# Attention of a two-layer transformer kernel: normalization of each score tile moved behind the next tile's row maxima, three PSUM regions for scores, one bank for transposes

## What is computed

```python
# layer 0: 16 heads of q, k, v; causal
scores = jnp.einsum('bhqd,bhkd->bhqk', q, k) * scale
scores = jnp.where(causal, scores, jnp.finfo(scores.dtype).min)
probs = jax.nn.softmax(scores, axis=-1)
attn = jnp.einsum('bhqk,bhkd->bhqd', probs, v)
# layer 1: 16 heads of q, one k and one v for all, no mask
scores = jnp.einsum('bhqd,bkd->bhqk', q, k) * SCALE
attn = jax.nn.softmax(scores.astype(jnp.float32), axis=-1)
out = jnp.einsum('bhqk,bkd->bhqd', attn, v)
```

## Time and profile before

| | us |
|---|---|
| device time, median of five runs | 13053.91 |
| the five runs | 12818.4 to 13098.67 |
| the profiled execution, device time | 12700.41 |
| its span on the slowest core (core 1) | 12698.9 |
| spans of the eight cores | 12643.5 to 12698.9 |
| attention of layer 0 (first scores to last cast of OT) | 1311.4 to 3442.6 |
| attention of layer 1 | 7126.6 to 9940.5 |

### The profile page before, as it was taken

One profiled execution on the slowest core, in us unless ns is written; L12 is line 12 of the kernel. 1 busy time (PEld: TensorE's weight loads), 2 busy tenths in 40 slices (PEclk: granted clock), 3 DMA queues, 4 the chain that ended last, 5 costly groups with the idle time before them and its releaser, 6 DMA issues. The chain is left out here.

```text
span 12698.9 us, 112380 instructions; the slowest of 8 cores (12643.5 to 12698.9 us)
## 1 busy us (share of the span) xinstructions
PE 7415.4 (58%) x35408; PEld 3432.6 (27%) x35408; DVE 4428.7 (35%) x8280; ACT 2475.1 (19%) x4202; POOL 135.0 (1%) x233
## 2 busy tenths in 40 slices
PE   1399433333379997281814644444444679997881
PEld 0144111111134443140412222222222334443340
DVE  4411444444414445708022344444444211111002
ACT  2100233333201112202121133333333000000000
POOL 0000000000000000000000000000000000000000
PEclk9999655555589998595956755555555789998995
DMA  1123000000132332141333100000000232223444
GB/s 50 48 55 57 19 7 7 10 7 7 28 86 48 59 60 44 36 81 35 72 118 104 35 7 7 7 7 6 5 7 4 45 78 50 53 52 78 93 90 165
DMA packets 426230, 581.35 MB, mean 46 GB/s; under 512 B 257200, under 2 KB 347312, under 8 KB 401456
## 3 DMA queue, kind: packets, MB, share of 16 engines
q0 software_dynamic: 75216, 237.39, 10.9%
q1 hardware_dynamic: 350432, 336.77, 8.3%
HBM read 655.71 MB, written 155.71 MB: 64 GB/s over the span
## 5 line engine op out<-in xcount | busy, mean ns | idle before, releaser
L636 PE MATMUL SCA<-P 128*128 128x512 bf16 x896 | 425.7, 559 | 1548.8 <-ACT P L86 1521.0
L86 DVE TENSOR_TENSOR P<-P 128x512 f32<-128x512 f32 (+6 forms) x700 | 691.4, 988 | 1674.3 <-DMA P<-g_hb 1603.0
L86 ACT ACTIVATE P<-SCA,st 128x1024 bf16<-128x1024 f32 (+1 forms) x512 | 515.8, 1007 | 3233.6 <-DVE st L86 3233.6
L781 PE MATMUL OT<-P 128*128 128x512 bf16 x1664 | 625.4, 555 | 734.3 <-DVE P L86 560.6
L607 PE MATMUL PP<-identS,P 128*128 128x128 bf16 x6656 | 732.3, 292 | 533.4 <-DVE P L86 532.6
L488 PE MATMUL QP<-P 128*128 128x512 bf16 x4224 | 961.2, 393 | 24.6 <-DMA P<-wqk 13.1
L607 PEld LDWEIGHTS PP<-identS,P 128*128 128x128 bf16 x6656 | 626.7, 134 | 854.7 <-issue 839.6
L86 DVE TENSOR_TENSOR st<-st 128x1 f32<-128x1 f32 x1632 | 259.4, 159 | 1404.4 <-ACT P L86 1214.1
L1160 PE MATMUL F1G<-P 128*128 128x512 bf16 x2816 | 627.4, 384 | 175.9 <-DVE P L86 117.2
L1250 PE MATMUL F1D<-P 128*128 128x512 bf16 x2816 | 619.2, 382 | 111.2 <-SPq L1215 111.2
L894 PE MATMUL F0P<-P 128*128 128x512 bf16 x2816 | 638.6, 380 | 67.3 <-DMA P<-w 67.3
(11 more groups left out here) (86 smaller groups left out, 6664.0 us busy)
## 6 DMA issues: line engine op xcount, KB each, us to landing
P<-w POOLq DMA_DIRECT2D x22, 2048.0 KB, 28.0
P<-w2p POOLq DMA_DIRECT2D x32, 1408.0 KB, 10.3
P<-wgu POOLq DMA_DIRECT2D x44, 1024.0 KB, 9.4
P<-wd POOLq DMA_DIRECT2D x32, 1408.0 KB, 10.2
P<-x SPq DMA_DIRECT2D x32, 1024.0 KB, 4.9
gn_hb<-P SPq DMA_DIRECT2D x176, 128.0 KB, 1.7
P<-gn_hb SPq DMA_DIRECT2D x176, 128.0 KB, 2.0
hf_h<-P SPq DMA_DIRECT2D x44, 512.0 KB, 6.0
```

What stands on the lines that cost most here:

```text
L86: ins = real(*args, **kw)
L636: ins = t.matmul(scslice(c, qt), QH[h % 2][:, qt * 128:(qt + 1) * 128], k.Bp[:, kbase + c * 512: kbase + c * 512 + 512], start=True, stop= ...
L781: ins = t.matmul(OT[:], VH[h % 2][:, kt * 128:(kt + 1) * 128], PT[:, kt * 512:(kt + 1) * 512], start=(kt == 0), stop=(kt == ktn - 1))
```

## The change

Four things are rewritten in `phase_att`, for both layers. The score regions: three PSUM tensors of two banks (SR0 to SR2) that are handed out in a ring, one per two chunks, so a tile of one or two chunks takes one region and one exponential, and a larger one two. PP is half as large, one bank, so each block of transposes waits until the block before it has been copied out. On DVE the sum, reciprocal and scaling are a function `do_rzpn`, called for tile qt - 1 after the maxima and `negm` of tile qt (of which there are two now), with the copy of block 1 of the same tile qt - 1 right behind it, and the cast of OT comes one tile later (qt % 4 == 1). On ACT the copy of block 0 of tile qt - 1 stands ahead of the exponential of tile qt.

```diff
-        negm = k.st1[:, 0:1]; za = k.st1[:, 1:2]; zb = k.st1[:, 2:3]
+        negm_b = [k.st1[:, 0:1], k.st1[:, 6:7]]
+        za = k.st1[:, 1:2]; zb = k.st1[:, 2:3]
...
-        def haf(qt):
-            n = nchf(qt)
-            return (n + 1) // 2, n - (n + 1) // 2
-
-        with self.nc.psum_tensor(f"SCA{L}", [128, 1024], F32) as SCA, \
-             self.nc.psum_tensor(f"SCB{L}", [128, 1024], F32) as SCB, \
-             self.nc.psum_tensor(f"PP{L}", [128, 2048], BF16) as PP, \
+        def nregf(qt):
+            return 1 if nchf(qt) <= 2 else 2
+
+        regs_of = {}
+        rr = 0
+        for h in range(HEADS):
+            for qt in range(NT):
+                n = nregf(qt)
+                regs_of[(h, qt)] = [rr, (rr + 1) % 3][:n]
+                rr = (rr + n) % 3
+
+        with self.nc.psum_tensor(f"SR0{L}", [128, 1024], F32) as SR0, \
+             self.nc.psum_tensor(f"SR1{L}", [128, 1024], F32) as SR1, \
+             self.nc.psum_tensor(f"SR2{L}", [128, 1024], F32) as SR2, \
+             self.nc.psum_tensor(f"PP{L}", [128, 1024], BF16) as PP, \
              self.nc.psum_tensor(f"OT{L}", [128, 512], F32) as OT:
-            pph = [PP[:, 0:1024], PP[:, 1024:2048]]
-
-            def scslice(c, qt):
-                ha, hb = haf(qt)
-                if c < ha:
-                    return SCA[:, c * 512:(c + 1) * 512]
-                return SCB[:, (c - ha) * 512:(c - ha + 1) * 512]
+            SCR = [SR0, SR1, SR2]
+
+            def scslice(h, qt, c):
+                rg = regs_of[(h, qt)][c // 2]
+                return SCR[rg][:, (c % 2) * 512:(c % 2 + 1) * 512]

             def transp(t, h, qt, ppq):
                 nkb = nchf(qt) * 4
                 PSB = PSBs[qt % 2]
                 k.wt(t, f"a{L}pn_{h}_{qt}")
                 for b in range((nkb + 7) // 8):
-                    half = b % 2
-                    if half in ppq:
-                        k.wt(t, ppq[half])
+                    if ppq:
+                        for m in ppq[0]:
+                            k.wt(t, m)
                     j0, j1 = b * 8, min(nkb, b * 8 + 8)
                     for j in range(j0, j1):
-                        ins = t.transpose(pph[half][:, (j - j0) * 128:(j - j0 + 1) * 128],
+                        ins = t.transpose(PP[:, (j - j0) * 128:(j - j0 + 1) * 128],
                                           PSB[:, j * 128:(j + 1) * 128], k.ident[:])
                     k.bump(ins, "sT", mark=f"a{L}tpb_{h}_{qt}_{b}")
-                    ppq[half] = f"a{L}pte_{h}_{qt}_{b}"
+                    nm = "S" if b % 2 == 0 else "V"
+                    ppq[:] = [[f"a{L}pte{nm}_{h}_{qt}_{b}"]]
                 k.marks[f"a{L}tp_{h}_{qt}"] = k.marks[f"a{L}tpb_{h}_{qt}_{(nkb-1)//8}"]
...
             def tenf(t):
-                ppq = {}
-                lastA = None
-                lastB = None
+                ppq = []
+                regfree = {}
                 for h in range(HEADS):
                     k.wt(t, f"a{L}qv_{h}")
                     for qt in range(NT):
-                        ha, hb = haf(qt)
+                        nch = nchf(qt)
                         kbase = h * 2048 if L == 0 else 0
-                        if lastA is not None:
-                            k.wt(t, lastA)
-                        for c in range(ha):
-                            ins = t.matmul(scslice(c, qt),
-                                           QH[h % 2][:, qt * 128:(qt + 1) * 128],
-                                           k.Bp[:, kbase + c * 512: kbase + c * 512 + 512],
-                                           start=True, stop=True)
-                            k.bump(ins, "sT", mark=f"a{L}scc_{h}_{qt}_{c}")
-                        lastA = f"a{L}expA_{h}_{qt}"
-                        if hb:
-                            if lastB is not None:
-                                k.wt(t, lastB)
-                            for c in range(ha, ha + hb):
-                                ins = t.matmul(scslice(c, qt),
+                        regs = regs_of[(h, qt)]
+                        for i, rg in enumerate(regs):
+                            if rg in regfree:
+                                k.wt(t, regfree[rg])
+                            for c in range(2 * i, min(nch, 2 * i + 2)):
+                                ins = t.matmul(scslice(h, qt, c),
                                                QH[h % 2][:, qt * 128:(qt + 1) * 128],
                                                k.Bp[:, kbase + c * 512: kbase + c * 512 + 512],
                                                start=True, stop=True)
                                 k.bump(ins, "sT", mark=f"a{L}scc_{h}_{qt}_{c}")
-                            lastB = f"a{L}expB_{h}_{qt}"
+                            regfree[rg] = f"a{L}exp_{h}_{qt}_{i}"
                         if qt > 0:
                             transp(t, h, qt - 1, ppq)
                             if (qt - 1) % 4 == 3:
                                 self._att_pv(t, L, h, (qt - 1) // 4, causal, VH, PT, OT)
...
+            def do_rzpn(v, h, qt):
+                nch = nchf(qt)
+                nreg = nregf(qt)
+                if nreg == 2:
+                    k.wt(v, f"a{L}exp_{h}_{qt}_1")
+                    ins = v.tensor_tensor(zs, za, zb, OP.add)
+                else:
+                    k.wt(v, f"a{L}exp_{h}_{qt}_0")
+                    ins = v.tensor_copy(zs, za)
+                k.bump(ins, "sV")
+                k.wtv(v, "sVa", k.cnt["sVa"])
+                ins = v.reciprocal(rz, zs)
+                k.bump(ins, "sV", mark=f"a{L}rz_{h}_{qt}")
+                k.wt(v, f"a{L}rz_{h}_{qt}")
+                PSB = PSBs[qt % 2]
+                ins = v.tensor_scalar_mul(PSB[:, 0:nch * 512], PSB[:, 0:nch * 512], rz)
+                k.bump(ins, "sV", mark=f"a{L}pn_{h}_{qt}")

             def vecf(v):
                 for h in range(HEADS):
@@ -663,12 +680,13 @@
                         off = qt % 4
                         for c in range(nch):
                             k.wt(v, f"a{L}scc_{h}_{qt}_{c}")
-                            sl = scslice(c, qt)
+                            sl = scslice(h, qt, c)
                             if causal and c == nch - 1:
                                 v.tensor_tensor(sl, sl, k.msk()[:, off * 512:(off + 1) * 512], OP.add)
                             ins = v.tensor_reduce(ngp[c], sl, AX, OP.max, negate=True)
                         k.bump(ins, "sV")
                         k.wtv(v, "sVa", k.cnt["sVa"])
+                        negm = negm_b[qt % 2]
                         if nch == 1:
                             ins = v.tensor_copy(negm, ngp[0])
                         elif nch == 2:
@@ -681,29 +699,16 @@
                             v.tensor_tensor(negm, ngp[2], ngp[3], OP.min)
                             ins = v.tensor_tensor(negm, negm, tmp, OP.min)
                         k.bump(ins, "sV", mark=f"a{L}neg_{h}_{qt}")
-                        ha, hb = haf(qt)
-                        if hb:
-                            k.wt(v, f"a{L}expB_{h}_{qt}")
-                            ins = v.tensor_tensor(zs, za, zb, OP.add)
-                        else:
-                            k.wt(v, f"a{L}expA_{h}_{qt}")
-                            ins = v.tensor_copy(zs, za)
-                        k.bump(ins, "sV")
-                        k.wtv(v, "sVa", k.cnt["sVa"])
-                        ins = v.reciprocal(rz, zs)
-                        k.bump(ins, "sV", mark=f"a{L}rz_{h}_{qt}")
-                        k.wt(v, f"a{L}rz_{h}_{qt}")
-                        PSB = PSBs[qt % 2]
-                        ins = v.tensor_scalar_mul(PSB[:, 0:nch * 512], PSB[:, 0:nch * 512], rz)
-                        k.bump(ins, "sV", mark=f"a{L}pn_{h}_{qt}")
                         if qt > 0:
-                            self._ptevac_v(v, L, h, qt - 1, nchf, pph, PT)
-                        if qt % 4 == 0 and qt >= 4:
+                            do_rzpn(v, h, qt - 1)
+                            self._ptevac_v(v, L, h, qt - 1, nchf, PP, PT)
+                        if qt % 4 == 1 and qt >= 5:
                             g = qt // 4 - 1
                             k.wt(v, f"a{L}pv_{h}_{g}")
                             ins = v.tensor_copy(k.A[:, h * 2048 + g * 512: h * 2048 + g * 512 + 512], OT[:])
                             k.bump(ins, "sV", mark=f"a{L}oev_{h}_{g}")
-                    self._ptevac_v(v, L, h, NT - 1, nchf, pph, PT)
+                    do_rzpn(v, h, NT - 1)
+                    self._ptevac_v(v, L, h, NT - 1, nchf, PP, PT)
...
             def scaf(sc):
                 for h in range(HEADS):
                     for qt in range(NT):
-                        ha, hb = haf(qt)
+                        nch = nchf(qt)
+                        regs = regs_of[(h, qt)]
                         PSB = PSBs[qt % 2]
+                        if qt > 0:
+                            self._ptevac_s(sc, L, h, qt - 1, nchf, PP, PT)
```

(21 more changed lines are left out.)

18 lines of the change are left out of this document (10 added, 8 removed).

## The result

The changed kernel took 13363.85 us (median of 6 runs, 13076.94 to 13610.18), the kernel before, beside it and earlier, 12974.72 (median of 10, 12670.45 to 13224.35). The ratio is 1.0294 with a 95% interval of 1.0172 to 1.0417. It became slower, as forecast (13460, range 13150 to 13620; 3.2% on the sum's own scale); the interval lies above 1, but it begins at 1.7%, so the times alone don't settle that the loss is over 2%.

A forecast was written before the change was run, and what follows sets the result against it. A loop of waits, not an engine, was taken to bound the attention stages. Layer 0's +163 us and layer 1's +249, together +412, added to the median 13053.9 gave 13466, rounded to 13460, range 13150 to 13620.

The forecast's parts named there:

- The removed wait: On DVE before the small operations: the 2.88 us wait for ACT's exponential becomes 0.17, -2.71 us per four-chunk tile.
- The new wait: On DVE before its copy: waiting out the same tile's transposes through one bank takes 3.77 us instead of 0.11, +3.66.
- The tile: In the attention loop, a four-chunk tile costs +0.95 us, making the layer 1 period 10.1 us; three chunks again +0.95.
- The third region off the path: On PE: the third score region removes a wait for ACT that had 4 us to spare, so gains nothing.
- The head's end: At each head's last tile, normalized alone: 6.6 us in layer 1, 7.8 in layer 0, so +4.4 and +5.6.
- The product: At the other three P V products of a layer 1 head: length unchanged, cast a tile later, +0.2 us each.
- The sum: Over both attention stages: layer 0 +163 us, layer 1 +249, together +412, or 13112 on the profiled scale, 3.2% more.
- The sign that I had named for a wrong forecast: In the profile after: a rising granted clock of the attention stages would show the forecast wrong.
- The rival in which PE wakes up: In both attention stages: PE at its faster level shortens transposes and products, total -168 us, 12532 profiled scale; chance 5%.
- The ring of banks pays: In attention: DVE's copy wait stays hidden, only removed waits count, -1127 us, 11573 on the profiled scale; chance 3%.
- The smaller loss: In attention: copy wait near 3.05 us, products at 5.4, about +172 us, 12872 on the profiled scale; chance 6%.
- the late scores: In attention tiles: the third chunk misses its 1.8 us slack, 1.5 us more per tile, +530, near 13990; chance 4%.

The follow-up runs named there:

- DVE's order put back: The changed kernel with DVE's scaling, copy and cast in their earlier order, one transpose bank kept: layer 0 2076.0 us, layer 1 2842.9, whole median 13122.61.
- two banks: The changed kernel with two transpose banks, two score regions and ACT's exponential ahead of its copy: layer 0 2304.0 us, layer 1 2678.5.
- the ring of two: The changed kernel with two score regions instead of three, nothing else: layer 0 2403.2 us, layer 1 3115.0, whole 13513.83 (median of two).
- the copy a tile later: Changed kernel with two transpose banks and score regions, two buffered score tiles, DVE's copy and product a tile later, scores ahead, undrained heads: 11503.73 us, ratio 0.868.

## Why the prediction was right

Point by point, by its own steps.

- The removed wait. I had -2.71 us a tile and DVE's waits for ACT nearly gone; 43.2 us are left of 1214.1. Right, but for a mis-sized 0.07 us: the sum of the two halves follows the small operations before it with no gap of 0.17 (four in one run at 8813.18), so the wait of 2.88 became the usual gap of 0.10 between instructions.
- The new wait. I had 3.77 us, added up from the earlier trace rows; it is 3.75 in the tile shown, and 1413.0 / 382 = 3.70 over all copies, of three chunks too (3.32 there, the 0.43 less that I had). One term has a slip that did no harm: eight transposes at 1.86 / 16 are 0.93 us and not 0.83, which would have made the sum 3.67. What eight more cost is 1.86 - 1.01 = 0.85 us, so 2.04 - 0.85 = 1.19 for the last step, and 8817.95 to 8819.14 is 1.19. DVE's order put back takes it away and restores 9.1 us a tile, two banks make 2.29 of it. Shown by both.
- The tile: +0.95 us forecast, period 10.1. It is 10.00 against 9.13, so +0.87, the 0.07 above less; the tile ahead of it in the same stretch took 10.18. For tiles of one and two chunks I had waits for scores of 1.4 and 1.85 us; they are 1.44 and 1.86.
- The third region off the path. Right for the gain that the change could hope for: PE's wait fell by 1387 us and no tile of layer 1 got shorter. But not for the new order, where it covers 0.1 us a tile in layer 1 and up to 1.7 in layer 0. With the ring of two those show.
- The head's end. I had a wait of 0.7 us for exponential 15, then 3.77 again. DVE's rows of the changed kernel at the end of a head of layer 1, which answer to the earlier trace rows:

```profile
9917.16 0.69 DVE L86 COPY P<-PP 128x1024 bf16<-128x1024 bf16 x1 [3.75 <-PE PP L614]
9918.60 0.16 DVE L86 TENSOR_TENSOR st<-st 128x1 f32<-128x1 f32 x1 [0.74 <-ACT P L86]
...
9919.27 0.75 DVE L86 TENSOR_SCALAR P<-P,st 128x2048 bf16<-128x2048 bf16 x1 [0.17 <-DVE st L86]
9923.77 0.69 DVE L86 COPY P<-PP 128x1024 bf16<-128x1024 bf16 x1 [3.75 <-PE PP L614]
9930.77 0.69 DVE L86 CAST P<-OT 128x512 bf16<-128x512 f32 x1 [6.30 <-PE OT L788]
```

  0.74 us for ACT, 3.75 for PE, and 9917.16 to 9923.77, copy to copy, is 6.61 (6.6 forecast, 2.2 before). At a head's start the third chunk is waited for 0.72 us (0.6 forecast).
- The product. I kept its length and added 0.2 us. In layer 1 the maxima behind it wait 5.9 to 6.6 us for scores, where the cast had waited 6.3 on average, and the cast comes a tile later without a wait. Right.
- The sum. +163 and +249 us forecast, +165 and +246 measured on core 1. So near a hit is in part luck: a group of four tiles with its product grew by 3.7 us on average in layer 1 (43.9 to 47.6 from cast to cast) where the terms give 4.0, and the start and end of a head took that back (8.1 us for what is left of a head, 7.55 by the terms). Layer 0's terms were not all read one by one. The time on the medians' scale, 13460, came out 96 us too high; 79 of that is the scale, since the kernel before, with five more runs, has a median of 12974.72 and not 13053.91. The nearness of a median is luck too: single times of either kernel lie over 530 us apart, more than the effect. What the forecast rests on is the 411 us of the stages.
- The sign that I had named for a wrong forecast, a granted clock that rises, was there in part: 0.63 in layer 1 after 0.58. It changed nothing on the path. Eight transposes still take 1.01 us at their usual pace, and the products' waits are as long as before. The rival in which PE wakes up fell with that; it had asked for about 0.88. The other sign, maxima that wait for scores, was badly put: they wait 690 us in all, but where the sum has it, behind products, in tiles of one and two chunks and at a head's start.
- The ring of banks pays: fell, and for the reason given. By the Trainium skill (Perfetto Trace Analysis, section Matmuls), independent groups of matmuls should rotate through PSUM banks so that the evacuation overlaps the next group's matmuls. The runs agree for the transposes: with one bank ACT's copy stands between two blocks and costs 1.46 us a tile where DVE waits for it. They also show what the rule leaves open: with the order put back the same single bank cost 29 us in a whole stage, since the evacuation was off the path.
- The smaller loss and the late scores fell: the copy waited 3.32 us or more in all of layer 0 and 3.64 or more in all of layer 1, and the maxima found their scores ready in the middle of a group of four-chunk tiles.

## What to carry to other kernels

A deferred step takes its consumers with it: when a scaling moves one tile later, the copy that needs its transposes must move too, or the engine pays PE's whole turn in the place of ACT's. Write down for each engine, for one period, what it produced last and what it asks for next; the ask should lie a period behind the thing asked for, on every engine. And buy PSUM banks where a wait stands on the path: here the third score region took away 1387 us of PE's waiting that no tile of layer 1 had paid for, and the bank it took from the transposes cost 1.46 us in each tile of four chunks once DVE waited for them.

## What the runs showed of the hardware

The same product of sixteen 128x512 matmuls took 5.90 us on average in layer 1 of the kernel before, 5.72 in the changed one (both core 1) and 3.84 in the one with the copy a tile later (core 5), with no change to it. The granted clock of that stage was 0.58, 0.63 and 0.68. One product of the kernel before and one of the changed one:

```profile
8797.75 5.88 PE L781 MATMUL OT<-P 128*128 128x512 bf16 x16 [7.97 <-DVE P L86]
```

```profile
8830.09 5.36 PE L788 MATMUL OT<-P 128*128 128x512 bf16 x16 [1.12 <-DVE P L86]
```

In the first, PE had stood idle for 8 us; in the second it had done two short blocks with gaps of 1.30 and 1.12 us. In both, the weight loads of the first nine or more matmuls start 0.43 us apart, the pace of the 1.2 GHz level, and the last ones run at the faster one. The product of 3.62 us ran near the level of 2.4 GHz. I hadn't counted on this.

What stood ahead of the fast product (scores, transposes and product, with one gap of 0.28 us) doesn't explain it by itself. Core 7 of the same execution has the same row of work, and its product is slow:

```profile
7502.16 1.91 PE L613 MATMUL PP<-identS,P 128*128 128x128 bf16 x16
7503.87 5.17 PE L788 MATMUL OT<-P 128*128 128x512 bf16 x16
7509.28 0.69 DVE L86 COPY P<-PP 128x1024 bf16<-128x1024 bf16 x1 [2.51 <-PE OT L788]
```

Its granted clock in the stage was 0.64 against 0.69 on core 1, its products took 4.63 us on average against 3.66, and its layer 1 took 1828.5 us against 1760.3. So once waits no longer pace the loop, the clock of a core shows in the time: 62 us more in 64 products, 68 in the stage. This also divides the 190 us by which the stage was shorter than my 1950. Core 7 is still 121 under it. By the pace of these two cores, products of 5.72 to 5.90 us would give some 1905 to 1920 us. So about 150 of the 190 come from the faster product and the rest from a stall that I had set too high. That is an estimate, stretched beyond the products that core 7 had; no run held the clock fixed.

In the profiled execution of the changed kernel the clock shows elsewhere. Cores 1 and 5 have spans 265 us apart, and none of that lies in attention, where both had the same granted clock (0.56 and 0.63) and the same lengths (2296.0 and 2296.7 us, 3059.8 and 3061.2). Between the two attention stages, where PE is the busiest engine, core 1 took 3879 us at 0.78 (PE busy for 2637) and core 5 took 3687 at 0.82 (2458). So two cores whose whole spans differ can still be compared stage by stage, if the clock of the stage is read beside its length.
